# A vision layer's attention: the matmuls of V are issued ahead of the products of a quad, and no longer behind the turns of its probabilities

## The reference

```
qkv = xw @ qkv_w.T + qkv_b            # windows of 64 tokens
attn = softmax(q * scale @ swap(k))   # scores, then probabilities
out = attn @ v                        # products
return out @ proj_w.T + proj_b        # projection
```

## Time and profile before

| | |
|---|---|
| median of 3 runs | 753.43 us (748.14 to 753.71) |
| the profiled execution | 753.32 us |
| its span, from the first to the last instruction | 751.6 us |
| mean granted clock of TensorE | 0.904 |
| TensorE busy with matmuls | 607.8 us (81%) |
| TensorE busy with weight loads | 409.5 us (54%) |
| VectorE busy | 524.1 us (70%) |
| ScalarE busy | 423.6 us (56%) |
| GpSimd busy | 347.6 us (46%) |

### The profile page before, as it was taken

How to read it: one execution, slowest core, us unless ns; L and a number is a source line. 1 busy time by engine, 2 the same in 40 slices (tenths; PEclk the granted TensorE clock), 3 DMA queues, 4 the chain that set the end, 5 groups by cost and what they waited for, 6 DMA issues and landing times. The chain is left out here.

```text
span 751.6 us, 17904 instructions
## 1 busy us (share of the span) xinstructions
PE 607.8 (81%) x6719; PEld 409.5 (54%) x6720; DVE 524.1 (70%) x951; ACT 423.6 (56%) x763; POOL 347.6 (46%) x534
## 2 busy tenths in 40 slices
PE   4794999999999999998630666160899999999994
PEld 3322788888888888887210322050555555555552
DVE  4895577677777777774598599377566667766662
ACT  3693576777767777766495444230355555555551
POOL 6203466677766777664482565411333333333330
PEclk9996799999999999999775897576799999999998
DMA  9301122211222111210200000000001101111101
GB/s 197 62 0 47 33 55 47 53 44 44 51 51 51 45 44 45 58 38 2 24 0 0 1 0 0 0 1 0 1 20 22 22 21 23 24 22 23 21 21 25
DMA packets 60323, 23.19 MB, mean 31 GB/s; under 512 B 43730, under 2 KB 60114, under 8 KB 60242
## 3 DMA queue, kind: packets, MB, share of 16 engines
q1 hardware_dynamic: 59424, 21.95, 14.2%
q10 hardware_dynamic: 690, 0.13, 0.1%
q0 software_dynamic: 128, 0.00, 0.0%
HBM read 5.29 MB, written 4.19 MB: 13 GB/s over the span
## 5 line engine op out<-in xcount | busy, mean ns | idle before, releaser
L687 DVE TENSOR_REDUCE top<-psum 128x16 f32<-128x1024 f32 x64 | 78.4, 1225 | 74.4 <-PE psum L515 74.4
L621 ACT ACTIVATE prob_t<-psum 128x512 f32<-128x512 f32 x128 | 69.7, 595 | 70.4 <-PE psum L528 70.3
L515 PE MATMUL psum<-k_st,q_st 64*128 64x256 f32 x512 | 75.4, 414 | 12.3 <-POOL q_st L473 9.5
L469 POOL TENSOR_TENSOR k_st<-raw,kc 128x256 f32<-128x256 f32 x128 | 75.9, 614 | 18.4 <-PE psum L515 11.8
L692 DVE TENSOR_TENSOR prob<-psum,top 128x1024 f32<-128x1024 f32 x64 | 78.4, 1224 | 2.2
L542 PEld LDWEIGHTS psum<-v_st,prob_t 128*64 128x64 f32 x2048 | 65.7, 139 | 22.8 <-issue 20.9
L613 ACT ACTIVATE prob<-prob 128x1024 f32<-128x1024 f32 x64 | 67.3, 1052 | 12.2 <-DVE prob L692 12.2
L542 PE MATMUL psum<-v_st,prob_t 128*64 128x18 f32 x2048 | 72.0, 213 | 1.5 <-ACT o_t L639 1.5
L1405 ACT ACTIVATE hid<-psum,b1c 128x512 f32<-128x512 f32 x96 | 62.5, 692 | 17.8 <-PE psum L1317 17.8
L1325 PE MATMUL psum<-x_t,w1x 64*64 64x256 f32 x1024 | 71.8, 397 | 0.0
L528 PE MATMUL psum<-kc,prob 128*128 128x128 f32 x512 | 70.0, 281 | 0.0
(11 more groups left out here) (186 smaller groups left out, 1308.0 us busy)
## 6 DMA issues: line engine op xcount, KB each, us to landing
raw<-big_bc SPq DMA_DIRECT2D x128, 64.0 KB, 2.4
h_all<-in_x SPq DMA_DIRECT2D x16, 256.0 KB, 5.2
x_st<-big_a SPq DMA_DIRECT2D x32, 128.0 KB, 2.2
out<-out_st SPq DMA_DIRECT2D x128, 32.0 KB
kc<-constants SPq DMA_DIRECT2D x1, 459.0 KB, 3.8
w1x<-in_L_ffn_W SPq DMA_DIRECT2D x2, 128.0 KB, 4.1
w2x<-in_L_ffn_W SPq DMA_DIRECT2D x1, 128.0 KB, 3.8
wraw<-in_L_tok_qkv_w ACTq DMA_DIRECT2D x2, 32.0 KB, 4.9
```

The costliest lines, as they stand in the source:

```text
L469: pool.tensor_tensor(k_st[:, f, b], k, m, ALU.mult).then_inc(k_masked, 1)
L515: m = pe.matmul(banks[hg][:, 256 * b:256 * b + 256], q_st[q, f, b, :], k_st[q, f, b, :, :], start=True, stop=True, skip_group_check=True)
L621: act.activation(prob_t[:, f, 4 * hg:4 * hg + 4, :].rearrange("p j q -> p (j q)"), banks[2 + hg][:, :], ACT.Copy).then_inc(prob_t_done, 1)
L687: dve.tensor_reduce(top[:, f, :], sc, AX.X, ALU.max).then_inc(top_done, 1)
```

## The change

In TensorE's body of a step, `values(i + 1)` moves from behind `turn(i, 1)` to a place right behind `scores(i + 1, 0)`, ahead of `products(i, par, 0)`. The function itself, its waits and all other engines' programs stay as they are.

```
                     if live(i, -1):
                         scores(i + 1, 0)
+                        values(i + 1)
                     if live(i, 0):
                         products(i, par, 0)
                         turn(i, 1)
-                    if live(i, -1):
-                        values(i + 1)
                     if live(i, 1):
                         turn_o(i - 1, 1)
```

## The result

The changed kernel took 786.24 us (median of 4 runs, 784.83 to 787.63) against 753.57 us (748.14 to 753.78): a ratio of 1.045, 95% interval 1.041 to 1.049. Run again later, the pair stood at 785.30 and 754.00, ratio 1.038 (1.033 to 1.043). The forecast was 789 us with a range of 781 to 796.

What follows compares the result with a forecast made beforehand. TensorE's own order in the attention stage was taken to set the pace; 27 steps each 1.33 us longer, less 0.4 us, gave 35.5 us on top of 753.3, so 789 us (+4.7%), range 781 to 796.

Steps and rivals of the forecast that it cites:

- The bound: Attention stage: TensorE's own order sets the pace at 8.60 us a step, and whatever makes it wait is paid in full.
- The wait: V of quads 5 to 31, 27 steps: held until ScalarE's u copy of the same step, a hole of 1.42 us.
- Rival A: V's wait already met by the u copy of the step before: no hole, 750.5 us; chance 4%.
- rival C: ScalarE's run comes earlier within the step, so half the hole might go: 771 us; chance 5%.
- The delay of the signal: From the end of ScalarE's u copy to V's start on TensorE: 0.14 us, bounded by zero and 0.28.
- The step: Attention step with the u wait: grows by 1.33 us, from 8.60 to 9.93 us.
- the tighter order: TensorE in attention, V no longer between turns of the probabilities and turn of o: gives back 0.09 us a step.
- The ramp: V of quads 1 to 4 moves without the wait: the order alone gives back 0.09 us each, 0.4 us.
- Behind attention: Scan and experts, the stages after attention: forecast as before, no change in time.
- the drain: Steps behind the last V: chained to TensorE, so nothing there absorbs the delay; no change of its own forecast.
- The next wait: Products waiting for ScalarE's late o_t copy: seen at about 0.91 us against a start at 1.07, fits with 0.16 to spare.
- Rival B: TensorE's granted clock falls in attention, with a hole of 1.4 us in each 9.9; chance 4%.

Runs made afterwards that it cites:

- the wait alone: Kernel before, V in its old place, with only a TensorE wait for the same step's u copy put ahead of the products: 798.80 us, ratio 1.059.

## Why the prediction was right, and where its sizes were off

**The bound.** Right: TensorE's order set the pace, and each wait added there was paid in full. Against the same order without a hole, a step was longer by the hole and 0.05 to 0.07 us more for holes from 0.71 to 1.89 us, and by 0.48 us for the hole of 0.30.

**The wait.** Right in place, count (27) and releaser. Moving that copy on ScalarE took the loss away, moving it half way took away 0.54 of 1.14 us a step, adding the wait without the move brought it back. So this wait as the cause is shown. Rival A (met already) is excluded by the 27 waits recorded, rival C (filled in part later) by steps that are all 9.74 or 9.75 us long. ScalarE's run from the probabilities to u takes 3.1 us as before. Whether V could be written into its half of bank 6 while ScalarE still reads u's half, no run here tried; every kernel here keeps the wait.

**Two readings of the code in it were off, without effect on the sum.** The prediction calls the u copy waited for that of quad i−3. The wait is for i−3 copies, so the last of them is that of quad i−4, as the code says of ScalarE's step i; "in this very step" is right. And the copy of the V before is not made in ScalarE's step before: `copy_v(i)` is in step i as well. It is met all the same, since it stands early in the step. In the changed kernel it ends at 207.22 + 0.81 = 208.03 and the next V starts at 212.58:

```profile
207.22 0.81 ACT L631 ACTIVATE v_st<-psum 64x256 f32<-64x256 f32 x2
...
212.58 0.69 PE L565 MATMUL psum<-w_v,x_st 128*64 128x64 f32 x16 [1.35 <-ACT u_all L665]
```

**The delay of the signal.** 0.14 forecast, 0.15 for V. For the products held by the u copy it was 0.05 (the wait alone); what sets the difference stays open.

**The step.** 9.93 forecast, 9.74 measured. The hole was right: from the scores to V it is 202.84 − 200.35 = 2.49 us, as forecast. (The forecast's 1.42 counts from the start that the products had, the row's 1.35 from the modelled end of the scores, 0.07 later.) The mis-sized term is the tighter order: 0.09 us forecast, 0.27 in the changed step (1.42 − 1.15) and 0.25 in the step without a hole (4.09 to 3.84). From V to the products I took the 0.62 that V's group holds ahead of the turn of o; it is 0.48 (202.84 to 203.32). Turn of o to scores is 0.31, not 0.34; products to turns 1.03, not 1.04. That is 0.18 of the 0.19 us, 5 us in all.

**The ramp.** 0.4 us forecast, 2.3 in this profile: 0.8 by the tighter order, which is the same mis-sized term, and most of the rest by a clock that rose early in this execution (1.00 from 83 us on) and late in a second one (from 89).

**Behind attention.** Nothing forecast; +3.3 us in this profile. The same code took 388.7 to 392.8 us across the profiles of this study; of two kernels that differ in nothing but the place of the u copy, one had 388.7 and one 392.8. Whether the change has any part in it stays open: the changed kernel's two profiles have 392.5 and 392.1. Against this profiled execution the forecast of 788.8 was 3.9 us too high: 5.1 by the step, 1.9 by the ramp, 0.4 by the drain, less the 3.3 here (with what rounding leaves). That the total came out so near is in part luck: the 3.3 us that nobody forecast made up for more than half of what the step was forecast too long.

**The next wait.** ScalarE's late o_t copy, forecast to fit with 0.16 us of room, held up nothing.

**Rival B, the clock.** It did not come at a hole of 1.35 us in this kernel, in two executions (granted 1.00 from 120 to 370 us in the first, from 120 to 375 us in the second). But I had put it too far off: a hole of nearly the same length ahead of the products (1.26 us), and one of 1.61 ahead of V, both brought it in some steps. The wait alone shows the granted clock swing from 1.00 to 0.50 and back, at 1.5 us for each step at the low clock (0.50 from 178.4 to 181.8 us in one of them); the changed kernel doesn't. The size was off too. My estimate for this rival came from the products, 1.90 us in the ramp, where the granted clock was 0.50, against 1.11, a factor of 1.71: with a third of TensorE's 8.6 us a step so slowed, a step takes 2.0 us more, 27 steps 55 us. The price was 9 us in the wait alone.

## What to carry to other kernels

A group of matmuls that moves takes its waits along: look for the one whose releaser runs in the same step, and compare the end of that releaser with the new start. Here the order was good (−0.25 us a step) and only the partner on ScalarE stood too late; moved together, the two beat the kernel before by 0.9% (746.14 us, ratio 0.991), and with V behind the products by 1.1% (744.99, ratio 0.989; no telling which of the two is better), while each alone gave nothing or a loss. What a group costs depends on what follows it: V held 0.62 us ahead of the turn of o and 0.48 ahead of the products.

## What was not expected of the hardware

In a loop that else runs at a granted clock of 1.00, three kernels with a hole in each step of about 10 us fell to 0.50 in single steps (one of each: 178.4 to 181.8 us, 161 to 163, 355 to 357), for 1.5 to 1.6 us more in each: six of 27 steps with the wait alone (a hole of 1.26 us, the products right behind it), four with 1.61 us ahead of V, three with 1.89. The changed kernel, with 1.35 ahead of V, had none in two executions (1.00 from 120 to 370 and from 120 to 375 us). What decides between them stays open.
